# The gate's scaling of the last two chunks on VectorE, and the longest head pair last in each turn of the last stage

## The reference, cut to what matters

```python
xn = layernorm(x)                         # x: 8 samples, 4096 tokens, 1024 features
k, q, v = split(xn @ W_kqv.T)             # 16 heads of 64
score = q @ k.T / 32 + slope[h] * (n - s) # ALiBi: bias grows with the key's place n
s = softmax(score) @ v
out = xn                                  # gate network, 3 cycles
for _ in range(3):
    tf = sigmoid(gelu(gelu(gelu(out @ w1) @ w2) @ w3) @ w4)
    coupling = 0.1 + ar * (0.7 * gf + 0.3 * tf - 0.5) * 2
    out = out + coupling * twist(out)     # twist([a, b, c, d]) = [c, -d, -a, b]
x = x + s * silu(out)
```

## Time and profile before

| What | us |
|---|---|
| Three runs: lowest, median, highest | 1507.23, 1531.64, 1618.33 |
| The profiled execution | 1515.8 |
| Its span on the slowest core, core 4 | 1514.3 |
| ACT busy, PE busy, DVE busy in it | 1333.5, 1375.8, 791.3 |
| First exp of the attention | 577.7 |
| Spans of the other cores | 1500.0 to 1512.9 |

### The profile page before, as it was taken

The page is one execution under the profiler, slowest core; times in us unless marked ns, Lnnn a source line. Parts: engine busy times, 40 slices in busy tenths (PEclk is TensorE's granted clock), DMA queues, the critical chain, the costliest instruction groups (busy, mean ns, idle before and its releaser), DMA issues.

```text
span 1514.3 us, 49494 instructions; the slowest of 8 cores (1500.0 to 1514.3 us)
## 1 busy us (share of the span) xinstructions
PE 1375.8 (91%) x18227; PEld 945.6 (62%) x18394; DVE 791.3 (52%) x1863; ACT 1333.5 (88%) x2009; POOL 50.5 (3%) x105
## 2 busy tenths in 40 slices
PE   1779899999999998899999999999999899999996
PEld 1667688888888866455764444565554444655554
DVE  4675777877878894322223333333333444434666
ACT  1455788878888877999999999999999999999998
POOL 2331000000000000000000000000000000000000
PEclk9988899999999999999999999999999999999999
DMA  8852031132132116411122121122331122222433
GB/s 185 206 185 64 2 111 59 57 105 65 57 96 74 57 57 156 102 34 34 34 48 47 47 62 44 44 52 74 69 65 55 53 66 69 55 61 75 117 104 112
DMA packets 122535, 115.58 MB, mean 76 GB/s; under 512 B 8384, under 2 KB 106944, under 8 KB 121920
## 3 DMA queue, kind: packets, MB, share of 16 engines
q1 hardware_dynamic: 118848, 101.26, 22.6%
q0 software_dynamic: 3456, 11.14, 5.0%
HBM read 89.96 MB, written 33.55 MB: 82 GB/s over the span
## 4 chain that ended last, share of the span: by engine, by line
PE 80%; issue 5%; DVE 5%; ACT 4%; DMA 4%; DVEq 1%; SPq 0%; ACTq 0%
PE PS L804 20%; PE PS L825 18%; PE PS L535 14%; PE PS L551 11%; PE PS L635 9%; PE PS L630 4%; DMA XT<-x 4%; ACT PB L937 3%; PE PS L563 3%; DVE ACC L1548 2%; DVE SST L1566 1%; PE PS L576 1%; PE PS L505 0%; DVE stat L1205 0%; DVE QT L1366 0%
## 5 line engine op out<-in xcount | busy, mean ns | idle before, releaser
L937 ACT ACTIVATE PB<-PS 128x1024 bf16<-128x1024 f32 (+2 forms) x1088 | 908.7, 1027 | 12.1 <-PE PS L804 10.3
L804 PE MATMUL PS<-QT,KT 64*128 64x256 bf16 x3888 | 372.4, 272 | 35.6 <-ACT PB L937 17.4
L825 PEld LDWEIGHTS PS<-VB,PB 128*128 128x128 bf16 x7776 | 273.8, 97 | 166.9 <-issue 164.9
L825 PE MATMUL PS<-VB,PB 128*128 128x66 bf16 x7776 | 343.5, 193 | 24.9 <-DVE ACC L1548 22.6
L804 PEld LDWEIGHTS PS<-QT,KT 64*128 64x128 bf16 x3888 | 147.1, 94 | 258.9 <-issue 233.0
L535 PE MATMUL PS<-XB,W 128*128 128x256 bf16 x1536 | 217.2, 285 | 0.0
L551 PE MATMUL PS<-H,W 128*128 128x256 bf16 x1536 | 180.8, 276 | 1.0 <-ACT H L862 0.7
L1548 DVE COPY ACC<-PS 128x264 f32<-128x264 f32 x128 | 55.3, 432 | 228.4 <-PE PS L825 228.0
L535 PEld LDWEIGHTS PS<-XB,W 128*128 128x128 bf16 x1536 | 154.7, 102 | 22.9
L551 PEld LDWEIGHTS PS<-H,W 128*128 128x128 bf16 x1536 | 150.5, 99 | 21.8 <-issue 2.5
L635 PE MATMUL PS<-XB,WQ 128*128 128x512 bf16 x398 | 126.9, 378 | 11.2 <-DVE QT L1366 2.8
(11 more groups left out here) (99 smaller groups left out, 1219.9 us busy)
## 6 DMA issues: line engine op xcount, KB each, us to landing
XT<-x SPq DMA_DIRECT2D x32, 512.0 KB, 5.5
XF<-x SPq DMA_DIRECT2D x32, 512.0 KB, 7.2
g_s<-TY SPq DMA_DIRECT2D x32, 512.0 KB, 3.9
GS<-g_s SPq DMA_DIRECT2D x128, 128.0 KB, 2.6
XS<-x SPq DMA_DIRECT2D x128, 128.0 KB, 2.8
out<-SST SPq DMA_DIRECT2D x128, 128.0 KB, 1.9
WKV<-wkv POOLq DMA_DIRECT2D x8, 512.0 KB, 7.7
WQ<-wq POOLq DMA_DIRECT2D x8, 256.0 KB, 11.8
```

Of the source, the lines that this page charges most:

```text
L804: x = TE.matmul(BANK[2 * (g % 3) + b % 2][:, (b // 2) * 256:(b // 2 + 1) * 256], KT[i][hh * 64:(hh + 1) * 64, (nt - KT0[i]) * 128:(nt - KT ...
L825: x = TE.matmul(BANK[6][:, (2 * hh + j) * VW:(2 * hh + j + 1) * VW], PB[g % NPB][:, col_of(b) + j * 128:col_of(b) + (j + 1) * 128], vbv[i] ...
L937: x = SE.activation(out=dst[:, k, t], in_=src[:, k, t], func=AF.Exp, bias=-MARGIN, scale=1.0 / 32.0)
```

## The change

The operand order of the last stage is changed, so that i = 7 (3 blocks) comes first in a turn and i = 6 (29 blocks) last. For tiles 28 to 31 `scale_x` is a DVE function: two `tensor_scalar` instructions (multiply by a scalar of the partition, add another) in place of two activations. It runs in operations G 0 and G 2 right ahead of `add_twist`, both tiles of a chunk together, with a drain before it (G 0 only) and one behind it. ACT no longer does it, and `add_twist` waits for no ACT step there. `tanh_y` stays where it was, on ACT ahead of groups 14, 15, 36 and 37.

```diff
-STAGES = [..., ((6, 0), (5, -12), (7, 0))]
+STAGES = [..., ((7, 0), (5, -12), (6, 0))]
...
         for g in range(NG):
-            if g in (8, 9):
-                scale_x(2 * E14 + g - 8)
             if g in (14, 15):
                 tanh_y(2 * E14 + g - 14)
-            if g in (28, 29):
-                scale_x(2 * E15 + g - 28)
...
+        def scale_x(t):
+            k = t % 2
+            VE.wait_ge(sXF[k], 16 * (t // 2 + 1))
+            VE.wait_ge(sGst[k], 16 * (t // 2))
...
+            VE.tensor_scalar(out=tv[:, 0:4:3, :], in0=xv[:, 0:4:3, :], scalar1=f[4], scalar2=f[10],
+                             op0=AOP.mult, op1=AOP.add)
+            VE.tensor_scalar(out=tv[:, 1:3, :], in0=xv[:, 1:3, :], scalar1=f[4], scalar2=f[11],
+                             op0=AOP.mult, op1=AOP.add)
...
         def add_twist(t):
...
-            VE.wait_ge(aYa, t + 1)
+            if t < 2 * E14:
+                VE.wait_ge(aYa, t + 1)
...
             elif op == ("G", 0):
+                VE.drain()
+                scale_x(2 * E14)
+                scale_x(2 * E14 + 1)
+                VE.drain()
                 add_twist(2 * E14)
                 add_twist(2 * E14 + 1)
                 gate_scalars(E15)
...
             elif op == ("G", 2):
+                scale_x(2 * E15)
+                scale_x(2 * E15 + 1)
+                VE.drain()
                 add_twist(2 * E15)
                 add_twist(2 * E15 + 1)
```

More of the change, by code:

```diff
@@ L33 @@
 PAIRS = [5, 7, 2, 6, 3, 1, 4, 0]
-STAGES = [((0, 0),), ((1, 0), (2, 0)), ((3, 0), (4, 0), (5, 4)), ((6, 0), (5, -12), (7, 0))]
+STAGES = [((0, 0),), ((1, 0), (2, 0)), ((3, 0), (4, 0), (5, 4)), ((7, 0), (5, -12), (6, 0))]
 NV0 = 3
@@ L1322, in gate_scalars @@
             VE.tensor_tensor(out=f[:, :, 10:12], in0=f[:, :, 8:10], in1=m, op=AOP.mult).then_inc(vFs, 1)
+        def scale_x(t):
+            k = t % 2
+            VE.wait_ge(sXF[k], 16 * (t // 2 + 1))
+            VE.wait_ge(sGst[k], 16 * (t // 2))
+            xv = XF[k].rearrange("p (b f) -> p b f", b=4)
+            tv = TY[k].rearrange("p (b f) -> p b f", b=4)
+            f = [fin[:, 12 * k + j:12 * k + j + 1] for j in range(12)]
+            VE.tensor_scalar(out=tv[:, 0:4:3, :], in0=xv[:, 0:4:3, :], scalar1=f[4], scalar2=f[10],
+                             op0=AOP.mult, op1=AOP.add)
+            VE.tensor_scalar(out=tv[:, 1:3, :], in0=xv[:, 1:3, :], scalar1=f[4], scalar2=f[11],
+                             op0=AOP.mult, op1=AOP.add)
         def add_twist(t):
```

## The result

The kernel became slower by 1.02% (ratio 1.0102, 95% interval 1.0076 to 1.0127), or about 15 us, and its median time lies above the range that I gave. Twenty executions of each went from 1517.66 to 1627.65 (median 1541.49) after and from 1506.39 to 1618.33 (median 1531.24) before.

A forecast was written before the change was run, and what follows sets the result against it. ACT was taken to bound the attention from 600 us on, PE from 577 to 600. 1515.8 - 1.4 (gate) - 2.3 (end) + 0.3 (order before the end) = 1512.4 us, 0.22% less; range 1499.5 to 1534.

The forecast's parts named there:

- What bounds the kernel: Attention from 577 us on: ACT is full from 600 us to the end, PE sets the pace between 577 and 600.
- DVE's price: Each new fp32 tensor_scalar of 128x512 in G 0 and G 2: 0.48 us from start to start, other end 0.66.
- G 0 and G 2: At the gate, tanh of tile 28 waits 0.3 us (0.1 gained), tanh of tile 30 waits 1.5 (1.3 gained).
- The sum of the gate: Scaling of tiles 28 to 31 moved from ACT to DVE: 1.4 us gained in all, bounds 0 and 5.6.
- The end: Behind the last exp: only one N (1.96 us gained) and a last group of one block; together 2.3 us gained.
- The order before the end: Last stage: job ends closer at its start and projections due earlier; 0.3 us lost, bounds 0.5 gained and 2 lost.
- the same ring, turned by one job: Last stage: same jobs in every turn, same cyclic sequence, boundaries and uneven groups equal in number.
- Rival 3: Start of the last stage: four ACC buffers force an N before an O; up to 7.8 us, 1519.9 total; chance 0.13.
- The sign that I had named: Around the start of the last stage, ACT's waits for scores growing by more than 4 us would show the prediction wrong.
- Due rounds: Projections for the last stage due by rounds 436 and 447 (was 451): 160 pieces in 176 rounds, 2% more.

The follow-up runs named there:

- run 9: Kernel before plus the gate's scaling on DVE, old order, tanh unmoved, and 20 unused matmuls on PE ahead of group 39's scores; ratio 0.9982 to before.
- run 1: Kernel before with only the new order of the last stage, the gate as before; ratio 1.0086 to the kernel before.
- run 3: Changed kernel, both edits, with the planner putting Ns earlier in DVE's list from job 92 on (gap 2 blocks, not 8); ratio 1.0014 to before.
- run 6: Kernel before, both edits absent, with the planner limited to three ACC buffers from job 90 on, so Ns precede most Os; ratio 1.0082 to before.
- run 2: Changed kernel with the old order of the last stage, so only the gate's scaling on DVE; ratio 1.0001 to the kernel before.
- run 4: Kernel before plus the gate's scaling on DVE, old order, tanh ahead of groups 15, 16, 39 and 40; ratio 0.9972 to before.
- run 7: Kernel before with exps of groups 240, 300, 360, 420 repeated one to four times; no ratio; one repeat cost 1.12 us on five cores, 1.85 to 2.05 on three.

## Why the prediction was wrong

The forecast was 0.22% less; measured was 1.02% more. By the steps of the prediction:

- **What bounds the kernel.** Right: ACT in the attention, PE before 600 us. Incomplete in one point. "So an ACT instruction taken away from there is worth its own time, unless a wait comes in its place" leaves out that a wait can cost more than itself.
- **DVE's price.** 0.48 us from start to start forecast, 0.46 measured.
- **G 0 and G 2.** The waits forecast at tanh were 0.3 and 1.5 us, the measured ones 0.27 and 1.52. Tanh of tile 30 came 0.55 us earlier than before (27.95 against 28.50 us after V7, core 2), where the forecast had 1.4 gained. Part of that is at G 0: tanh of tile 28 came 4.43 us after V7 in place of 4.08, so 0.35 later, where I had it 0.1 earlier. Then came the step that I did not have: PE idle 2.66 us, its clock halved, about 2 us lost (run 9). The sum of the gate was put at 1.4 gained; it was 0.6 to 1.2 lost. That no wait of ACT costs more than itself was an assumption that I never wrote down.
- **The end.** 2.3 forecast, 2.0 measured, by the mechanism given.
- **The order before the end.** This is the step that failed. "Every turn still has the same jobs, and the sequence is the same ring, turned by one job" is true of PE and ACT. It is not true of DVE's list, which a rule with memory writes. I put it at 0.3 us lost with a bound of 2; it was 14.5 lost. Rival 3 named the mechanism, the N forced in front of an O by four `ACC` buffers, and its place. It was given 0.13 and 7.8 us, and the ground against it was that all turns but the first have the old spacing. They have, but the lag of four made in the first turn did not shrink in the long job's gap: the planner saw no free gap, and twenty Os in a row (93 to 112) stood behind an N, five times the four that I had counted. The sign that I had named came too: ACT's waits for scores alone grew from 8.7 to 16.2 us.
- **Due rounds.** Projections moved earlier as worked out. Runs 1 and 3 have them, and up to O 88 they cost nothing.

How the 14.5 us divide between waits for the copy and the halved clock can be bounded. Behind O 103 the clock did not fall on any of the six cores, so the 4.0 us there are waits alone; core 0, columns as above:

```profile
1418.00:1500.00 82.00, 69.79 (x1039) 40.72 (x1052) 51.94 (x192) 78.22 (x103) 0.00 (x0) 1.00 0.39 113
```

Between O 88 and O 103 it fell two or three times on each core. In this stage one fall cost about 1.0 us in run 3, 1.4 in run 6 and 1.5 in run 1 (two for 2.9). By this estimate 2 to 4.5 of the 10.5 us up to O 103 are the clock's, and the waits are the larger part. A filler on PE in front of these waits, which would show it directly, was not run.

## What to carry to other kernels

A step moved to a faster engine gains nothing if it moves from well ahead of its use to right in front of it; move the use as well (from run 2 to run 4, tanh one and three groups later turned 0.6 us lost into 3.7 gained). If a planner writes an engine's order by a rule that depends on its own past, write out the new list before trusting that an order is "the same but turned"; look for long work standing in front of a short step that frees a resource. And price a gap on TensorE at more than its length, once its clock falls behind it.

## What the runs showed of the hardware

TensorE's granted clock fell to 0.50 after an idle time of 1.31 us on three of eight cores, and after one of 1.75 us on seven of eight (run 7), in a stretch where PE was busy over 90% of the time; in the kernel before it fell on two of eight cores after 1.43 us near tile 30 (cores 0 and 6). So one length of gap can go either way. It came back after some 3 to 7 us in most places. Twenty matmuls in the idle time (2.22 us) kept it at 1.00 and saved about 2 us (run 9). A tensor_scalar with two pointer scalars, fp32, 128x512 between SBUF operands took 0.54 us against 0.75 of the scalar_tensor_tensor of the same size (kernel after, 605.60 and 607.58).
